# Turning the shift rows of a top-k attention head: products and copies before, transfers of the SP queue after

## What is computed

```python
scores = jnp.einsum('bhqd,bhkd->bhqk', q, kk) * scale
vals, idx = jax.lax.top_k(scores, k)          # k = 32
w = jax.nn.softmax(vals, axis=-1)
vg = jnp.take_along_axis(v[:, :, None, :, :], idx[..., None], axis=3)
out = jnp.einsum('bhqk,bhqkd->bhqd', w, vg)
```

## Time and profile before

| | us |
|---|---|
| median of 3 runs | 31025.67 (30994.74 to 31053.72) |
| the profiled execution | 31029.18, of which the span is 31027.1 |
| DVE busy | 27113.2 (87%) |
| PE busy (matmuls) | 25435.5 (82%) |
| ACT busy | 23763.4 (77%) |
| POOL busy | 19632.6 (63%) |
| copies at L436 | 896, 470.3 us |
| products at L307 | 3200, 348.8 us |

### The profile page before, as it was taken

The page is one execution under the profiler, slowest core; times in us unless marked ns, Lnnn a source line. Parts: engine busy times, 40 slices in busy tenths (PEclk is TensorE's granted clock), DMA queues, the critical chain, the costliest instruction groups (busy, mean ns, idle before and its releaser), DMA issues. The chain is left out here.

```text
span 31027.1 us, 621399 instructions
## 1 busy us (share of the span) xinstructions
PE 25435.5 (82%) x191144; PEld 11618.2 (37%) x191145; DVE 27113.2 (87%) x155048; ACT 23763.4 (77%) x28857; POOL 19632.6 (63%) x7792
## 2 busy tenths in 40 slices
PE   7968877788888888888857888788888887888868
PEld 5743333333333333333323333333333333333322
DVE  6769899998989898989868989898999898999975
ACT  2238887788888888988827989798888887898833
POOL 0027776677777767777706777677777776777710
PEclk8989998899999989999968999899999898999979
DMA  1010000000000000000010000000000000000011
GB/s 47 13 66 6 6 5 6 5 6 5 6 6 6 6 5 6 6 6 6 5 62 23 6 6 6 6 6 5 6 6 6 5 6 5 6 6 6 5 39 58
DMA packets 125487, 383.03 MB, mean 12 GB/s; under 512 B 24964, under 2 KB 83220, under 8 KB 110040
## 3 DMA queue, kind: packets, MB, share of 16 engines
q1 hardware_dynamic: 118968, 324.00, 3.2%
q10 hardware_dynamic: 2432, 12.85, 0.1%
HBM read 207.77 MB, written 129.00 MB: 11 GB/s over the span
## 5 line engine op out<-in xcount | busy, mean ns | idle before, releaser
L232 POOL TENSOR_SCALAR Z<-S,M 128x3136 uint8<-128x3136 f32 (+1 forms) x2240 | 18390.0, 8215 | 6158.8 <-PE banks L336 5796.4
L510 DVE MAX8 C<-S 128x8 f32<-128x98 f32 x102400 | 19758.1, 252 | 1931.8 <-ACT S L421 1788.7
L421 ACT COPY S<-banks 128x896 f32<-128x896 f32 (+1 forms) x12800 | 10266.9, 820 | 1936.2 <-DVE C L510 673.0
L451 ACT ACTIVATE W<-banks 128x1024 f32<-128x1024 f32 (+1 forms) x9524 | 9796.2, 1029 | 1716.2 <-PE banks L336 1650.5
L327 PE MATMUL banks<-Q,K 99*128 99x512 bf16 (+2 forms) x22550 | 6433.5, 370 | 2667.2 <-ACT S L421 1407.7
L289 PE MATMUL banks<-K,Q 96*128 96x448 bf16 x22400 | 6577.1, 371 | 1457.6 <-ACT W L451 554.4
L372 PE MATMUL banks<-W,V 128*32 128x512 f32 (+1 forms) x45100 | 6840.7, 586 | 108.9 <-ACT W L454 78.9
L336 PE MATMUL banks<-NEG,Z 128*128 128x128 bf16 (+1 forms) x56300 | 6027.2, 224 | 0.0
L336 PEld LDWEIGHTS banks<-NEG,Z 128*128 128x128 fp8e4 x56300 | 4596.7, 101 | 1765.5 <-issue 263.2
L336 PE MATMUL banks<-NEG,ZA 128*128 128x128 bf16 (+1 forms) x24150 | 4782.3, 223 | 0.0
L327 PEld LDWEIGHTS banks<-Q,K 99*128 99x128 bf16 (+1 forms) x22550 | 1635.5, 99 | 7457.9 <-ACT S L421 3618.0
(11 more groups left out here) (219 smaller groups left out, 17005.0 us busy)
## 6 DMA issues: line engine op xcount, KB each, us to landing
K<-k_parts SPq DMA_DIRECT2D x130, 147.0 KB
Q<-q_parts SPq DMA_DIRECT2D x130, 147.0 KB
q_parts<-pj_parts SPq DMA_DIRECT2D x24, 784.0 KB, 4.7
k_parts<-pj_parts SPq DMA_DIRECT2D x24, 784.0 KB, 7.7
V<-v_rows SPq DMA_DIRECT2D x130, 112.5 KB, 7.5
v_rows<-pj_vt SPq DMA_DIRECT2D x8, 1800.0 KB, 11.8
att<-OS SPq DMA_DIRECT2D x772, 18.0 KB
K<-k_parts SPq DMA_DIRECT2D x130, 98.0 KB
```

What stands on the lines that cost most here:

```text
L232: pool.tensor_scalar(mask_at(tile)[0:rows, :].bitcast(U8), m.S[0:rows, slot(tile), :], m.M8[0:rows, side(i), t, 31:32], None, ALU.is_lt).t ...
L421: act.copy(m.S[0:rows, slot(tile), at:at + CW * w].rearrange("p (a n) -> p a n", a=w), m.AB[0:rows, pair(score_at[a]):pair(score_at[a]) + ...
L451: ins = act.activation(m.W[:, e % 4, 0:n_banks, :], m.AB[:, b:b + n_banks, :], ACT.Exp)
L510: ins = dve.max(m.C[0:rows, tile % 2, TOP_AT + k:RANKED:CHUNKS], m.S[0:rows, slot(tile), CHUNK * k:CHUNK * k + CHUNK])
```

## The change

The products at L307 and the copies at L436 are removed. SP now waits for the parts of a set (`maxp`), issues for each tile and each part one transfer that takes 128 single bf16 values from 128 partitions of `P` and writes them side by side into one row of `Q`, and then waits until all have landed (`turned`). That is 12 transfers for a set of 512, 3 for the small set, 75 for a head. PE's first unit of a set and POOL's reuse of `P` wait for `turned`.

```diff
@@ block.sync
+            def shift_rows(i, g):
+                k = max_sets(i) + g
+                sp.wait_ge(maxp, k + 1)
+                for j, t in enumerate(set_tiles(g)):
+                    rows, at = tile_rows(t), QW * g + 128 * j
+                    for a in range(3):
+                        sp.dma_start(m.Q[MAX_AT + a:MAX_AT + a + 1, side(i), at:at + rows],
+                                     m.P[0:rows, k % 2, a, j:j + 1]).then_inc(turned, 16)
+                sp.wait_ge(turned, 48 * turns(i, g))
+
+            ahead = 0
             for s, (i, g) in enumerate(sets):
+                while ahead < len(sets) and (ahead <= s + 1 or first_unit[ahead] <= fold_at[s] + PAIRS_):
+                    if sets[ahead][0] >= 0:
+                        shift_rows(*sets[ahead])
+                    ahead += 1
                 sp.wait_ge(os_done, s + 1)
...
                     load(i + 2)
+            if n:
+                for g in range(PENDING, SETS):
+                    shift_rows(n - 1, g)
@@ block.gpsimd, shift_parts
-                    pool.wait_ge(max_mm, k - 1)
+                    pool.wait_ge(turned, 48 * turns(*divmod(k - 2, SETS)))
@@ block.tensor
-            def shifts(i, g):
...
-                for j, t in enumerate(set_tiles(g)):
-                    rows = tile_rows(t)
-                    mm = pe.matmul(maxima[:, 128 * j:128 * j + rows], m.P[0:rows, k % 2, :, j],
-                                   m.identb[0:rows, 0:rows], start=True, stop=True)
-                mm.then_inc(max_mm, 1)
...
-                    pe.wait_ge(max_in, max_sets(i) + g + 1)
+                    pe.wait_ge(turned, 48 * turns(i, g))
...
-                    if e + 5 in first_unit and e + 5 < NE and sets[units[e + 5][0]][0] >= 0:
-                        shifts(*sets[units[e + 5][0]])
@@ block.scalar
-            def shift_rows(i, g):
-                k = max_sets(i) + g
-                act.wait_ge(max_mm, k + 1)
-                act.copy(m.Q[MAX_AT:MAX_AT + 3, side(i), QW * g:QW * g + set_width(g)],
-                         maxima[:, 0:set_width(g)]).then_inc(max_in, 1)
...
-                if x + 4 in first_unit and x + 4 < NE and sets[units[x + 4][0]][0] >= 0:
-                    shift_rows(*sets[units[x + 4][0]])
```

More of the change, by code:

```diff
@@ L118, in attend @@
     names = ("q_in", "v9_in", "v1_in", "a_mm", "a_ev", "s_free", "tops", "step", "found", "viol", "flag_mm", "flag_in",
-             "z_dve", "z_act", "z_pool", "part", "maxp", "max_mm", "max_in", "e_mm", "e_exp", "pv", "o_ev", "fold_mm", "os_done", "o_out")
+             "z_dve", "z_act", "z_pool", "part", "maxp", "turned", "e_mm", "e_exp", "pv", "o_ev", "fold_mm", "os_done", "o_out")
     with semaphores(nc, *names) as sems, nc.Block() as block:
         (q_in, v9_in, v1_in, a_mm, a_ev, s_free, tops, step, found, viol, flag_mm, flag_in,
-         z_dve, z_act, z_pool, part, maxp, max_mm, max_in, e_mm, e_exp, pv, o_ev, fold_mm, os_done, o_out) = sems
+         z_dve, z_act, z_pool, part, maxp, turned, e_mm, e_exp, pv, o_ev, fold_mm, os_done, o_out) = sems
         psO, psX = bank[6], bank[7]
         flags = psX[32:33, :]
-        maxima = psX[MAX_AT:MAX_AT + 3, :]
         TILES = NT * n
@@ L193, in max_sets, with turns @@
             return SETS * i
+        def turns(i, g):
+            return NT * i + set_tiles(g)[-1] + 1
         @block.sync
@@ L297, in flag @@
                 pe.matmul(flags[:, at], m.ones[:, 0:1], m.VI[:, at], start=True, stop=True).then_inc(flag_mm, 1)
-            def shifts(i, g):
-                k = max_sets(i) + g
-                pe.wait_ge(maxp, k + 1)
-                if k >= 1:
-                    pe.wait_ge(max_in, k)
-                for j, t in enumerate(set_tiles(g)):
-                    rows = tile_rows(t)
-                    mm = pe.matmul(maxima[:, 128 * j:128 * j + rows], m.P[0:rows, k % 2, :, j],
-                                   m.identb[0:rows, 0:rows], start=True, stop=True)
-                mm.then_inc(max_mm, 1)
             def fill(e):
@@ L406, in _ @@
             if n:
-                for g in range(PENDING, SETS):
-                    shifts(n - 1, g)
                 flag(n - 1, len(CHECKS) - 1)
@@ L490, in _ @@
                     folded(s)
-            if n:
-                for g in range(PENDING, SETS):
-                    shift_rows(n - 1, g)
         @block.vector
```

1 line of the change is left out of this document (removed).

## The result

The kernel after takes 37616.17 us, median of 4 runs (37566.93 to 37627.01), against 31031.1 us before: 1.212 times as long, with an interval from 1.210 to 1.214. The forecast was 31304 us with a range up to 32270. The side was right; the size was missed by 6312 us.

A forecast was written before the change was run, and what follows sets the result against it. DVE fullest, nearly level with the PE-ACT loop that sets the pace where DVE runs dry. Waits 444 + clock 132 + block ends 85 - gain 383 = +278 us, giving 31304 us; range 30750 to 32270, own range 31100 to 31650.

The forecast's parts named there:

- 1.5 us from the last issue to landing: SP's transfers: landing follows the last issue by 1.5 us, so a set of 512 takes 12 x 0.50 + 1.5 = 7.5 us.
- The issue: SP's cost to issue one transfer, taken as 0.50 us, with a range from 0.28 to 1.19 us.
- the gain: Removing ACT's copies and the idle time before them: two thirds of 574 us counted, 383 us, range 200 to 574.
- the clock: PE's longer waits bring stretches at the lower clock level: 1.1 us in each of 120 heads, 132 us.
- dear transfers: Rival: issue or processing takes 1.0 us a transfer, a set 13.7 us; +1816, 32840 us; chance 0.15.
- point of 0.83 us a transfer: Issue time from which the sets turned right after a store would be late too, 12 issues + landing exceeding 11.5 us.
- upper bound 0.9 us: Issue time behind the range's upper end: +1317 less the covered 72, 32270 us.
- Which sets are exposed: Set 1, turned behind store and loads, makes PE wait 4.3 us in 120 heads; most other sets cost PE nothing.
- margin of 3.2 us: Mean time from V9's landing to PE's first unit of set 1 in 120 heads, against 7.5 us of work.
- DVE's share of the loop swallows a third: ACT's saved time counts nearly whole where the PE-ACT loop sets the pace, not where DVE does: 383 of 574 us.
- cover: ACT's ready work hides 0.6 us of each set 1 wait of PE, leaving 3.7 us in 120 heads, 444 us.
- Block ends: SP turns three sets behind a block's last store, 19.4 us against 14.1: 5.3 us for 16 blocks, 85 us.

The follow-up runs named there:

- the spread rows: The changed kernel with its three shift rows in partitions 96, 100 and 104 instead of 96 to 98, product over 105 rows: 31948.04 us, ratio 1.031.

## Why the prediction was wrong, point by point

**The step that failed: "1.5 us from the last issue to landing".** The issue was well taken (0.60 us for 0.50). The landing was taken from one transfer at a time and added once to the set, as if nothing but the issues set the pace of the transfers before the last. Another rate does: each further transfer adds 1.54 us to the set and not 0.60, so it is 19.65 us, not 7.5. The kernel with one part, whose set happens to be 7.3 us, came out at 31519 us, 215 above the forecast; that it is so near is partly luck, for the gain and the clock below were both taken too small and partly cancel. The other 6097 us of the miss lie between that kernel and the kernel after, and the spread rows alone give back 5668.

**The rival "dear transfers" named the mechanism** ("128 separate values all go to one partition"), and its point of 0.83 us a transfer holds: at 1.54 us 680 of the 768 sets of 512 are late. Its price holds as well where a set is as long as it took it: for 13.7 us it had 325 late sets and 32840 us, and the kernel with two parts, at 13.5 us, has 326 and 32849 us (again with a gain and a clock that are both too small). It was priced at 1.0 us because L1457's issue was the dearest row, and the upper bound 0.9 us of the range was the same reading. Neither row writes single 2-byte values side by side into one partition. Where no row is near, the bound was not one.

**Which sets are exposed was right.** Set 1 alone is late up to 10.0 us a set (120 times in both kernels); with 19.65 us, 680 are. By the prediction's margin of 3.2 us a set 1 would be 16.5 us late; set by set the trace has 2018 us in 120 waits, 16.8 us each. The other 560 waits are 5.5 us each in the mean, where rows 6 alone give 1.36 + 19.65 - 12.85 = 8.2.

**The gain was mis-sized:** 383 us taken, 568 measured, the upper end. The argument that DVE's share of the loop swallows a third was wrong, or PE's products, counted at nothing, were worth something; the run took both away and cannot tell.

**What a wait costs beyond itself was mis-sized.** The prediction gave +1.1 us for the clock and -0.6 for cover. The kernel with one part lies 1075 us over the one that turns nothing. Its waits are 556 us and its block ends some 80 (23.5 us from the last store to the next product, 18.4 before, 16 times); 440 are left, 3.7 us for each wait. It is not the transfers as such, since the kernel with one part and early transfers lies only 18 us over the one that turns nothing. The kernel with spread rows gives nearly the same: 1504 us over it, less 906 of waits and some 182 of block ends (29.8 us after the last store), are 3.5 us for each of its 120 waits. The windows of the kernel after behind the wait shown above, a set 4 and so one wait of the 680, show where it can go (columns as in rows 2):

```profile
4427.60:4429.60 2.00, 2.00 (x11) 1.25 (x12) 0.00 (x0) 0.08 (x1) 1.71 (x6) 0.50 0.00 0
4429.60:4432.00 2.40, 2.40 (x5) 0.29 (x4) 0.00 (x0) 0.95 (x1) 2.40 (x1) 0.50 0.00 0
4432.00:4436.00 4.00, 4.00 (x22) 2.43 (x21) 2.28 (x14) 2.98 (x4) 4.00 (x1) 0.50 0.01 2
4436.00:4440.00 4.00, 3.65 (x27) 1.30 (x24) 3.73 (x24) 2.95 (x4) 3.11 (x8) 0.87 0.02 4
```

After 6 us of idle time PE runs for 8.4 us at the lower level, 1.2 GHz. It is busy throughout, and ACT does 4.0 us of work where at its 92% it would do 7.7. That is 3.7 us, against the 1.1 read from a wait of 2.47 us. Two things weaken this reading. ACT's first exponential begins 1.9 us after PE, so a part of it is the start of the loop and not the clock. And the level was 0.50 already from 4420.0, while PE was still busy, 1.6 us before it ran dry; that the wait brought the whole stretch is not shown. That the two figures of 3.7 us agree may be chance.

**Block ends.** The step was right in form. SP's and PE's rows at one block's end in the kernel after:

```profile
8364.02 16.03 SPq L227 DMA_DIRECT2D att<-OS  x2
8381.24 40.96 SPq L216 DMA_DIRECT2D Q<-P  x27
...
8428.75 0.13 PEld L310 LDWEIGHTS banks<-K,Q 96*128 96x128 bf16 x2 [49.53 <-issue]
```

The last store ends at 8380.05, and the next block's first product follows 48.7 us later; before it was 18.4 (7258.01 - 7239.65). In the median of the blocks it is 48.9 us after and 18.4 before, so this end is an ordinary one. 30.3 us in 16 blocks are 485 us, where the forecast had 85; by its own sum with sets of 19.65 us it would be 44.3 - 14.1 = 30.2 us.

**The sum again, with what was measured,** from the kernel that turns nothing, 30444 us: waits 5075, block ends 485, and 37616 - 30444 - 5560 = 1612 us left. PE was busy 27072.6 us against 24867.1 there, with the same products, at a mean clock of 0.816 against 0.915. That the rest is the clock is argued from these two numbers and the windows, not shown by a run of its own, and no run parts it from the slow instruction loads. It is 2.4 us for each of 680 waits, less than the 3.5 and 3.7 where only set 1 waits; why was not tested.

## What to carry to other kernels

A chain of small transfers has two rates (here 0.60 and 1.54 us a transfer), that of issue and that of landing, and a landing time read from a single transfer says nothing of the second: measure several of the very form, element size and destination, before building on them. Turning columns of 2-byte values into rows by DMA paid here in two cases, both with the transfers started as soon as the data was there: three rows 4 partitions apart, 1.5% under the turning by PE and ACT, and one row with four transfers a set instead of twelve, 1.8% under it, with two parts left out. Early transfers into three neighbouring rows were still 0.9% slower. Ask also what a slow transfer holds up that never waits for it.

## What the runs showed of the hardware

- Single 2-byte values written side by side by DMA into partitions 96 to 98, or 64 and 96, share one rate of 12 ns a value, over however many transfers they are spread (7.3, 13.5 and 19.65 us for four, eight and twelve of 128); 4-byte values into the same rows keep up with the issues (2.0 us to landing against up to 7.4). The Trainium skill, "DMA: Bandwidth & Descriptors", section "Specifications", says that transfers under 512 B do a read-modify-write. That might be the mechanism, but here it costs only the 2-byte values, and no run shows it directly.
- Column to column, 2 bytes a value, goes at the rate of issue (twelve in 9.23 us, at 0.60 us an issue); into one row of HBM it is the slowest form of all (25.61 us).
- With such slow writes behind every store, the packets of instruction loads on other queues took 1.9 and 2.8 times as long; by an estimate, 541 us less 118 at block ends, that cost 1.4% of this kernel's time.
- PE's granted clock stayed at 0.50, 1.2 GHz, for 8.4 us behind one wait of 6 us.
